# One row in 128 of an attention block given to POOL, and the masked-score pass one row earlier

## The chip, the cores and the metric

The kernel runs on one core of a Trainium2 chip. The metric is device time in microseconds of one execution, as the median of several runs. The engines are TensorE (PE in the profile), VectorE (DVE), ScalarE (ACT) and GpSimd (POOL); SyncE (SP) issues the DMAs.

## The reference

Four graph layers run one after the other on 8 graphs of 2048 nodes with 128 features, each with a residual and a layer norm. Layers 0, 2 and 3 multiply by a normalised adjacency matrix of 2048x2048. Layer 1 is the costly one, an attention whose score is a sum over features of a ReLU of a sum:

```python
q = x @ WQ
k = x @ WK
h = jax.nn.relu(q[:, None, :, :] + k[:, :, None, :])
score = jnp.einsum('bijd,d->bij', h, p)
att = jax.nn.softmax(score + mask, axis=-1)      # mask: 0 where adj > 0, else -1e22
return jnp.matmul(att, x)
```

For each graph and each of the 2048 rows i, a whole array of 128 features by 2048 nodes j must be formed (q plus one column of k, ReLU) and summed over the features with the weights p.

## The kernel before

The features lie on the 128 partitions, the nodes j along the free dimension. A graph is a batch b, and its rows i go in 16 blocks t of 128. A block has 32 groups g, and a group has four rows u, 128x2048 elements each. A group belongs to one engine: 20 groups of a block to VectorE (kind "D", line 658, a maximum of `q_pair` and one column of `k_pair`), 12 to ScalarE (kind "A", line 446, a ReLU of `q_f32` plus a column of `k_f32`). Groups 0, 1, 3, 4, 6, 8, 9, ... 28, 30 are VectorE's; groups 2, 5, 7, ... 29, 31 are ScalarE's.

`q_pair` holds two half-precision numbers in the place of one float, a high and a low part of q times |p|; the maximum is taken on the pair as one float. Each engine writes into a ring of two groups (`ring`). TensorE (line 891) sums each finished group over the partitions into `score` in PSUM, four chunks of 512 columns, with 32 multiplications for a D group and 16 for an A group. `rows_ready` counts finished groups, `rows_used` groups that TensorE is done with, so that an engine may write its group n+2 only when TensorE has used group n.

When the last group (31) of a block has been multiplied, VectorE reads the scores: `masked_scores` (lines 597 to 614) makes four passes (line 608, one for each chunk) that add the mask, which lies in `att`, and take the row maximum; then `row_max` (612) and `neg_max` (614). `bank_scored` counts the chunks that TensorE has finished, `scores_read` the chunks that VectorE has read. TensorE may start the next block's group 0 in a chunk only when it was read. ScalarE waits for `neg_max` ahead of its exponential (line 428), which stands ahead of its group 5. TensorE turns the weights at groups 4, 8, 12 and 16 (line 783), ScalarE and, in the tail only, VectorE copy them, and TensorE multiplies them by x at groups 10, 14, 18 and 22 (line 864). VectorE forms the next mask at group 24 (595), the inputs of the layer norm at group 26 (624 to 635) and the output at group 30 (639). Between those two POOL takes the root (`att_root`, lines 368 and 370).

The order within the engines is written out by hand. The pass over block t-1's scores stands inside block t, at a place given as (group, row):

```python
MASKED_AT, EXP_AT, NORM_AT, OUTPUT_AT = (1, 2), 5, 26, 30
```

so VectorE writes the four rows of group 0 and two of group 1, then reads the scores, then goes on. The first block of a batch has no such pass, and the last block's is in `att_tail`.

Of the kernel before, what the change touches and what calls it, by code (L numbers as in the profile page):

```python
# [9 lines left out]
ALU = mybir.AluOpType  # L10
# [19 lines left out]
def build(nc, x, adj, w0, b0, wq, wk, p, w2, b2, w3, b3, out):  # L30
# [31 lines left out]
    with ExitStack() as ctx:  # L62
        def sb(name, shape, dt=F32):
            return ctx.enter_context(nc.sbuf_tensor(name, shape, dt))

        def sem(name):
            return ctx.enter_context(nc.semaphore(name))
# [42 lines left out]
        rstd = sb("rstd", [P, PER])  # L110
        plus_half = sb("plus_half", [P, 1])
        ones = sb("ones", [P, 2])
        norm2 = sb("norm2", [P, 2])
        bound2 = sb("bound2", [P, 1])
        bound = sb("bound", [P, 1])
# [60 lines left out]
        rows_used = {"D": sem("vector_rows_used"), "A": sem("scalar_rows_used")}  # L176
        scores_read = sem("scores_read")
        mask_loaded = sem("mask_loaded")
        mask_ready = sem("mask_ready")
        bank_scored = sem("bank_scored")  # L180
        row_max_ready = sem("row_max_ready")
# [44 lines left out]
        TURN_AT = {4 + 4 * c: c for c in range(CHUNKS)}  # L226
        COPY_AT = {8 + 4 * c: c for c in range(CHUNKS)}
        MULTIPLY_AT = {10 + 4 * c: c for c in range(CHUNKS)}
        MASKED_AT, EXP_AT, NORM_AT, OUTPUT_AT = (1, 2), 5, 26, 30
        MASK_AT = 24  # L230

        def turned_beside(s):

# [103 lines left out]
        @block.gpsimd  # L337
        def _(pool):
            pool.memset(ident[:], 0.0).then_inc(ident_cleared, 1)
            pool.wait_ge(ident_cleared, 1)  # L340
            pool.affine_select(out=ident[:], in_=ident[:], compare_op=ALU.not_equal, fill=1.0, base=0,
                               pattern=[[-1, P]], channel_multiplier=1).then_inc(ident_ready, 1)
            pool.wait_ge(minus_half_ready, 1)
            pool.wait_ge(bound_ready, 2)
            pool.tensor_tensor(bound[:], bound2[:], plus_half[:], ALU.pow).then_inc(bound_ready, 1)
            pool.wait_ge(weights_loaded, 16 * 8)

            def graph_layer(b, stage, proj, xs, name):

                for k in range(2):  # L350
                    pool.wait_ge(turn_full[k], turn_use(b, proj, TURN_PROJ))
                for s in range(STEPS):
                    for j in range(PER):
                        t = s * PER + j
                        ins = pool.tensor_tensor(xs[:, t, :], xs[:, t, :], bias[name][:], ALU.add)
                    ins.then_inc(residual_biased, 1)
                for s in range(STEPS):
                    w = step_of(b, stage, s) + 1
                    pool.wait_ge(moments_ready, w)
                    settle(pool)  # L360
                    pool.tensor_scalar(var_eps[:], moments[:, :, 1], EPS, None, ALU.add).then_inc(variance_ready, 1)
                    pool.wait_ge(variance_ready, w)
                    pool.tensor_tensor(rstd[:], var_eps[:], minus_half[:, 0:PER], ALU.pow).then_inc(rstd_ready, 1)  # L363

            def att_root(n):
                pool.wait_ge(att_moments_ready, n)
                settle(pool)
                pool.tensor_scalar(att_var[:], att_mom[:, 1:2], EPS, None, ALU.add).then_inc(att_variance_ready, 1)  # L368
                pool.wait_ge(att_variance_ready, n)
                pool.tensor_tensor(att_rstd[:], att_var[:], minus_half[:, 0:1], ALU.pow).then_inc(att_rstd_ready, 1)  # L370

            with pool.Fori(0, B) as b:
                pool.wait_ge(degrees_ready, b + 1 + AHEAD)
                for i in range(GRAPH):
                    pool.tensor_tensor(dis[:, i, :], deg_sum[:, i, :], minus_half[:], ALU.pow).then_inc(roots_ready, 1)
                graph_layer(b, "layer0", "proj0", xin, "l0")
                with pool.Fori(1, T + 1) as t:
                    att_root(b * T + t)
                graph_layer(b, "layer2", "proj2", xatt, "l2")
                graph_layer(b, "layer3", "proj3", xatt, "l3")  # L380

# [127 lines left out]
        def _(dve):  # L509
# [87 lines left out]
            def masked_scores(n):  # L597

                dve.wait_ge(mask_ready, n)
                for c in range(CHUNKS):  # L600

                    if c < CHUNKS - 1:
                        dve.wait_ge(bank_scored, n * (CHUNKS - 1) + (c + 2 - CHUNKS))
                    else:
                        dve.wait_ge(rows_used[KIND[-1]], scored(n))
                    settle(dve)
                    part = att[:, c * BANK:(c + 1) * BANK]
                    nc.vector.tensor_tensor_reduce(out=part, in0=score[:, c, :], in1=part,  # L608
                                                   scale=1.0, scalar=-3.0e38, op0=ALU.add, op1=ALU.max,
                                                   accum_out=bank_max[:, c:c + 1]).then_inc(scores_read, 1)  # L610
                dve.wait_ge(scores_read, n * CHUNKS + CHUNKS)
                nc.vector.tensor_reduce(row_max[:], bank_max[:], AX.X, ALU.max).then_inc(row_max_ready, 1)
                dve.wait_ge(row_max_ready, n)
                nc.vector.tensor_scalar(neg_max[:], row_max[:], -1.0, None, ALU.mult).then_inc(neg_max_ready, 1)  # L614
# [27 lines left out]
            def att_block(b, t, before):  # L642
                n = b * T + t
                for g in range(GROUPS):
                    if before and g == NORM_AT:
                        norm_inputs(b, t - 1)
                    if before and g == OUTPUT_AT:
                        att_out(b, t - 1)
                    if g == MASK_AT:
                        mask(n)  # L650
                    if KIND[g] == "D":

                        dve.wait_ge(rows_used["D"], n * N_OF["D"] + (RANK[g] + 1))
                        for u in range(P // QUAD):
                            if before and (g, u) == MASKED_AT:
                                masked_scores(n)

                            ins = nc.vector.tensor_scalar(ring["D"][:, RANK[g] % RING * 4 + u, :], q_pair[:],  # L658
                                                          k_pair[:, bass.ds(t * P + (QUAD * u + g), 1)], None, ALU.max)
                        ins.then_inc(rows_ready["D"], 1)  # L660
# [97 lines left out]
        def _(pe):  # L758
# [3 lines left out]
            for kind in "AD":  # L762
                pe.sem_inc(rows_used[kind], RING)
            pe.sem_inc(scores_read, CHUNKS)
            for ahead in (att_output, out_stored, degrees_ready):
                pe.sem_inc(ahead, AHEAD)
            pe.wait_ge(ident_ready, 1)
            pe.wait_ge(w0_loaded, 16)
# [100 lines left out]
            def att_block(b, t, before):  # L869
                n = b * T + t  # L870
                for g in range(GROUPS):
                    kind = KIND[g]
                    if before and g in TURN_AT:
                        if TURN_AT[g] == 0:
                            pe.wait_ge(exp_ready, n)
                        turn_weights(b, t - 1, TURN_AT[g])
                    if before and g in MULTIPLY_AT:
                        weigh(b, t - 1, MULTIPLY_AT[g])
                    pe.wait_ge(rows_ready[kind], n * N_OF[kind] + (RANK[g] + 1))
                    window = unit_window if kind == "D" else sign_window  # L880
                    for c in range(CHUNKS):
                        if g == 0:

                            pe.wait_ge(scores_read, n * CHUNKS + (c + 1))
                        for part in range(2 if kind == "D" else 1):
                            for u in range(P // QUAD):
                                row = ring[kind][:, RANK[g] % RING * 4 + u, :]
                                row = halves(row)[:, c * BANK:(c + 1) * BANK, part] if kind == "D" else \
                                    row[:, c * BANK:(c + 1) * BANK]

                                ins = nc.tensor.matmul(score[QUAD * u:QUAD * (u + 1), c, :],  # L891
                                                       window[:, QUAD - 1 - g:2 * QUAD - 1 - g], row,
                                                       start=(g == 0 and part == 0), stop=(g == GROUPS - 1 and (kind == "A" or part == 1)),
                                                       tile_position=(0, QUAD * u))
                        if g == GROUPS - 1 and c < CHUNKS - 1:
                            ins.then_inc(bank_scored, 1)
                    ins.then_inc(rows_used[kind], 1)
# [61 lines left out]
```

## Time and profile before

| | |
|---|---|
| median of 3 runs | 15444.7 us (15443.2 to 15445.18) |
| profiled execution | 15425.52 us |
| its span, first to last instruction | 15423.3 us |
| mean granted TensorE clock | 0.974 of full speed |
| busy: TensorE, VectorE, ScalarE, POOL | 86%, 91%, 83%, 5% of the span |

The profile comes from one execution. Each instruction has a start and a duration; a group is all instructions of one line, engine, operation and pair of tiles, with the time for which its engine stood idle just ahead of them and who released it. A row's duration can overlap the next one's. TensorE's f32 multiplications appear as two records each.

### The profile page before, as it was taken

Reading aid. Unit: us, or ns where it says so; the run is one execution under the profiler, and the core shown is the slowest. Engines: PE = TensorE matmul, PEld = TensorE weight load, DVE = VectorE, ACT = ScalarE, POOL = GpSimd, SP = SyncE. Lnnn points to the kernel's source line nnn. Section 1 sums busy time; section 2 is a strip of 40 time slices with the busy share of each in tenths; the row PEclk is TensorE's granted clock in tenths of the full one; section 3 lists DMA queues with packets and bytes.
Section 4 is the critical chain, followed back from the end, with each engine's and each line's share of the span. In section 5 each row is a group of like instructions: output and inputs, shape, how many; then the busy total and the mean of one; then the engine's idle time right before and its main releaser. Section 6 shows DMA issues by size and latency. Waiting matters only on the chain. (4 is left out here: it accounts for less than half of the span.)

```text
span 15423.3 us, 363837 instructions
## 1 busy us (share of the span) xinstructions
PE 13297.8 (86%) x152965; PEld 6323.3 (41%) x152965; DVE 13958.6 (91%) x14776; ACT 12757.3 (83%) x7764; POOL 773.4 (5%) x863
## 2 busy tenths in 40 slices
PE   7888888888888888888888888888888888888888
PEld 4333453334533355333553335433354333543335
DVE  7999779997799977999779997899978999789996
ACT  6999769996699966999669996699966999679995
POOL 0000000000000000000000000000000000000000
PEclk9999999999999999999999999999999999999999
DMA  2000120001200012000120002100021000210001
GB/s 98 13 10 13 67 86 13 10 13 67 86 13 13 10 72 80 13 13 10 76 77 13 13 10 82 71 13 13 13 87 63 13 13 13 95 54 12 12 12 53
DMA packets 128454, 579.53 MB, mean 38 GB/s; under 512 B 27536, under 2 KB 61328, under 8 KB 61328
## 3 DMA queue, kind: packets, MB, share of 16 engines
q1 hardware_dynamic: 126864, 554.28, 9.4%
q8 instruction: 1492, 24.44, 0.6%
q14 instruction: 98, 0.80, 0.0%
HBM read 411.63 MB, written 142.61 MB: 36 GB/s over the span
## 5 line engine op out<-in xcount | busy, mean ns | idle before, releaser
L658 DVE TENSOR_SCALAR big<-q_pair,supp 128x2048 f32<-128x2048 f32 x10240 | 12302.8, 1280 | 42.7 <-PE score L891 35.8
L446 ACT ACTIVATE big<-q_f,k_f 128x2048 f32<-128x2048 f32 x6144 | 11758.2, 1996 | 694.1 <-PE score L891 681.4
L891 PE MATMUL score<-big,unit_window 128*32 128x512 f16 x81920 | 5335.8, 399 | 1773.9 <-DVE big L658 1522.6
L891 PE MATMUL score<-big,sign_window 128*32 128x512 f32 x49152 | 5615.4, 597 | 0.0
L891 PEld LDWEIGHTS score<-big,unit_window 128*32 128x32 bf16 x81920 | 2157.2, 97 | 4926.1 <-DVE big L658 2111.5
L891 PEld LDWEIGHTS score<-big,sign_window 128*32 128x32 f32 x49152 | 1607.8, 111 | 3113.6 <-issue 2832.1
L828 PE MATMUL acc<-supp,big 128*128 128x128 f32 x12288 | 1445.9, 275 | 30.3 <-ACT supp L402 29.0
L828 PEld LDWEIGHTS acc<-supp,big 128*128 128x128 f32 x12288 | 1406.4, 192 | 34.7 <-ACT supp L402 19.9
L386 ACT ACTIVATE x_turned<-turn 128x512 f32<-128x512 f32 x64 | 38.6, 603 | 1028.8 <-PE turn L783 971.6
L368 POOL TENSOR_SCALAR att_var<-att_mom 128x1 f32<-128x1 f32 x128 | 146.3, 1143 | 12870.3 <-DVE att_mom L635 12870.3
L556 DVE TENSOR_TENSOR agg<-acc,supp 128x512 f32<-128x512 f32 x64 | 44.3, 692 | 654.6 <-PE acc L828 654.6
L864 PEld LDWEIGHTS acc<-xin,att_turned 128*128 128x128 f32 x4096 | 505.2, 194 | 314.0 <-issue 313.4
L864 PE MATMUL acc<-xin,att_turned 128*128 128x128 f32 x4096 | 599.5, 290 | 2.4 <-DVE att_turned L385 2.4
L783 PE MATMUL turn<-ident,att 128*128 128x128 f32 x2560 | 418.3, 288 | 76.6 <-DVE big L385 46.4
L783 PEld LDWEIGHTS turn<-ident,att 128*128 128x128 f32 x2560 | 278.8, 143 | 402.7 <-issue 339.6
L386 ACT ACTIVATE big<-turn 128x512 f32<-128x512 f32 (+1 forms) x256 | 151.9, 593 | 342.1 <-PE turn L783 341.9
L428 ACT ACTIVATE att<-att,neg_max 128x2048 f32<-128x2048 f32 x128 | 256.5, 2004 | 175.8 <-DVE neg_max L614 172.0
L608 DVE CUSTOM_DVE_ANT_0 att<-score,att 128x512 f32<-128x512 f32 x512 | 324.0, 684 | 40.4 <-PE score L891 35.5
L385 DVE COPY big<-turn 128x512 f32<-128x512 f32 (+1 forms) x256 | 175.7, 686 | 169.1 <-PE turn L783 169.1
L433 ACT ACTIVATE att_turned<-turn 128x512 f32<-128x512 f32 x496 | 286.6, 578 | 45.5 <-PE turn L783 45.5
L370 POOL TENSOR_TENSOR att_rstd<-att_var,minus_half 128x1 f32<-128x1 f32 x128 | 276.3, 2159 | 10.7
L805 PE MATMUL acc<-w_l,x_turned 128*128 128x128 f32 x768 | 140.2, 342 | 119.4 <-DVE x_turned L385 111.8
(98 smaller groups left out, 2868.9 us busy)
## 6 DMA issues: line engine op xcount, KB each, us to landing
att<-in_adj_dram SPq DMA_DIRECT2D x160, 1024.0 KB, 4.8
adj_turned<-big SPq DMA_DIRECT2D x128, 1024.0 KB, 11.3
big<-adj_turned SPq DMA_DIRECT2D x128, 1024.0 KB, 18.0
q_f<-in_adj_dram SPq DMA_DIRECT2D x32, 1024.0 KB, 10.3
q_pair<-in_adj_dram SPq DMA_DIRECT2D x32, 1024.0 KB, 10.1
k_f<-in_adj_dram SPq DMA_DIRECT2D x32, 1024.0 KB, 10.4
xin<-in_x_dram SPq DMA_DIRECT2D x128, 64.0 KB, 1.8
out_dram<-xatt SPq DMA_DIRECT2D x32, 256.0 KB, 2.9
```

The lines of the kernel that those rows point to most:

```text
L370: pool.tensor_tensor(att_rstd[:], att_var[:], minus_half[:, 0:1], ALU.pow).then_inc(att_rstd_ready, 1)
L385: return nc.vector.tensor_copy(dst, turn[0][:])
L386: return nc.scalar.activation(dst, turn[1][:], ACT.Copy)
L428: nc.scalar.activation(att[:], att[:], ACT.Exp, bias=neg_max[:], accum_out=row_sum[:]).then_inc(exp_ready, 1)
L433: nc.scalar.activation(att_turned[:, k, :], turn[k][:], ACT.Copy).then_inc(turn_free[k], 1)
L446: ins = nc.scalar.activation(ring["A"][:, RANK[g] % RING * 4 + u, :], q_f32[:], ACT.Relu, bias=k_f32[:, bass.ds(t * P + (QUAD * u + g), 1)])
L608: nc.vector.tensor_tensor_reduce(out=part, in0=score[:, c, :], in1=part, scale=1.0, scalar=-3.0e38, op0=ALU.add, op1=ALU.max, accum_out=ba ...
L658: ins = nc.vector.tensor_scalar(ring["D"][:, RANK[g] % RING * 4 + u, :], q_pair[:], k_pair[:, bass.ds(t * P + (QUAD * u + g), 1)], None, A ...
L783: ins = nc.tensor.transpose(turn[k][:, j * P:(j + 1) * P], src(j), ident[:])
L828: ins = nc.tensor.matmul(acc[k][:, j * P:(j + 1) * P], big[:, t, m * P:(m + 1) * P], supp[:, m, :], start=(m == 0), stop=(m == T - 1))
L864: ins = nc.tensor.matmul(acc[0][:, 0:D], att_turned[:, k, j * P:(j + 1) * P], xin[:, c * PER + j, :], start=(c == 0 and j == 0), stop=(c = ...
L891: ins = nc.tensor.matmul(score[QUAD * u:QUAD * (u + 1), c, :], window[:, QUAD - 1 - g:2 * QUAD - 1 - g], row, start=(g == 0 and part == 0) ...
```

## The change

Row 3 of group 1 is left out of VectorE's list and written by POOL with a tensor-scalar operation (a minimum with 3.0e38, then a maximum with the column) into the same place in the ring. POOL first copies the column of `k_pair` to `pool_column`. In blocks 1 to 15 it waits for the first of the four masked-score passes (`scores_read`) before it writes the row, and then for the ring's place (`rows_used`). POOL's `att_root` for block t-1 comes behind the row of block t. TensorE waits for POOL's row ahead of group 1. `MASKED_AT` is (1, 1) in place of (1, 2).

```diff
+        pool_column = sb("pool_column", [P, 1])
...
-        MASKED_AT, EXP_AT, NORM_AT, OUTPUT_AT = (1, 2), 5, 26, 30
+        MASKED_AT, EXP_AT, NORM_AT, OUTPUT_AT = (1, 1), 5, 26, 30
         MASK_AT = 24
+        POOL_ROW = (1, 3)
...
+            def row(b, t, before):
+                n = b * T + t
+                g, u = POOL_ROW
+                pool.wait_ge(pool_row_ready, n + AHEAD)
+                settle(pool)
+                pool.tensor_copy(pool_column[:], k_pair[:, bass.ds(t * P + (QUAD * u + g), 1)]) \
+                    .then_inc(pool_column_ready, 1)
+                pool.wait_ge(pool_column_ready, n + 1)
+                if before:
+                    pool.wait_ge(scores_read, n * CHUNKS + 1)
+                    settle(pool)
+                pool.wait_ge(rows_used["D"], n * N_OF["D"] + (RANK[g] + 1))
+                settle(pool)
+                pool.tensor_scalar(ring["D"][:, RANK[g] % RING * 4 + u, :], q_pair[:], 3.0e38, pool_column[:],
+                                   ALU.min, ALU.max).then_inc(pool_row_ready, 1)
...
-                with pool.Fori(1, T + 1) as t:
+                pool.wait_ge(low_written, b * STEPS + STEPS)
+                pool.wait_ge(high_written, b * STEPS + STEPS)
+                row(b, 0, False)
+                with pool.Fori(1, T) as t:
+                    row(b, t, True)
                     att_root(b * T + t)
+                att_root(b * T + T)
...
+                            if (g, u) == POOL_ROW:
+                                continue
...
                     pe.wait_ge(rows_ready[kind], n * N_OF[kind] + (RANK[g] + 1))
+                    if g == POOL_ROW[0]:
+                        pe.wait_ge(pool_row_ready, n + 1 + AHEAD)
```

## Rows read from the trace of the kernel before


**Rows 1.** The page, part 1: busy time of each engine.
```profile
PE 13297.8 (86%) x152965; PEld 6323.3 (41%) x152965; DVE 13958.6 (91%) x14776; ACT 12757.3 (83%) x7764; POOL 773.4 (5%) x863
```

**Rows 2.** The page, part 5: groups; busy, mean ns | idle before, releaser.
```profile
L658 DVE TENSOR_SCALAR big<-q_pair,supp 128x2048 f32<-128x2048 f32 x10240 | 12302.8, 1280 | 42.7 <-PE score L891 35.8
L446 ACT ACTIVATE big<-q_f,k_f 128x2048 f32<-128x2048 f32 x6144 | 11758.2, 1996 | 694.1 <-PE score L891 681.4
...
L608 DVE CUSTOM_DVE_ANT_0 att<-score,att 128x512 f32<-128x512 f32 x512 | 324.0, 684 | 40.4 <-PE score L891 35.5
```

**Rows 3.** Timeline of VectorE, one block: start, us, line, operation [idle before].
```profile
2728.01 0.68 DVE L608 CUSTOM_DVE_ANT_0 att<-score,att 128x512 f32<-128x512 f32 x1
2728.62 0.08 DVE L608 DVE_READ_ACCUMULATOR2_ANT bank_max<- 128x1 f32 x1
...
2730.76 0.15 DVE L614 TENSOR_SCALAR neg_max<-row_max 128x1 f32<-128x1 f32 x1
2730.88 50.33 DVE L658 TENSOR_SCALAR big<-q_pair,supp 128x2048 f32<-128x2048 f32 x42
2781.49 14.44 DVE L658 TENSOR_SCALAR big<-q_pair,supp 128x2048 f32<-128x2048 f32 x12 [0.28 <-PE score L891]
...
2807.78 0.18 DVE L635 BATCH_NORM_AGGREGATE att_mom<-att_stats 128x2 f32<-128x6 f32 x1 [0.15 <-DVE att_stats L632]
2808.00 9.66 DVE L658 TENSOR_SCALAR big<-q_pair,supp 128x2048 f32<-128x2048 f32 x8
...
2817.83 12.04 DVE L658 TENSOR_SCALAR big<-q_pair,supp 128x2048 f32<-128x2048 f32 x10
2829.79 0.68 DVE L608 CUSTOM_DVE_ANT_0 att<-score,att 128x512 f32<-128x512 f32 x1
```

**Rows 4.** Waits of VectorE, the loop of the second batch (15 blocks).
```profile
DVE big L658 <- PE score L891: 4.5, 15, 0.3
```

**Rows 5.** Timeline of TensorE, end of the block before 2728.01.
```profile
2718.44 4.57 PE L891 MATMUL score<-big,sign_window 128*32 128x512 f32 x32
...
2724.65 3.63 PE L891 MATMUL score<-big,sign_window 128*32 128x512 f32 x32
```

**Rows 6.** Timeline of ScalarE around two masked-score passes.
```profile
2723.20 7.70 ACT L446 ACTIVATE big<-q_f,k_f 128x2048 f32<-128x2048 f32 x4 [4.99 <-PE score L891]
2730.94 2.01 ACT L428 ACTIVATE att<-att,neg_max 128x2048 f32<-128x2048 f32 x1
...
2832.73 2.00 ACT L428 ACTIVATE att<-att,neg_max 128x2048 f32<-128x2048 f32 x1 [1.69 <-DVE neg_max L614]
```

**Rows 7.** Timeline of TensorE ahead of the gap at 2781.49.
```profile
2766.91 2.00 PE L891 MATMUL score<-big,unit_window 128*32 128x512 f16 x32 [0.52 <-DVE big L658]
...
2779.32 3.99 PE L891 MATMUL score<-big,unit_window 128*32 128x512 f16 x64
```

**Rows 8.** Groups of POOL by shape; columns as in rows 2.
```profile
L368 POOL TENSOR_SCALAR att_var<-att_mom 128x1 f32<-128x1 f32 x128 | 146.3, 1143 | 12870.3 <-DVE att_mom L635 12870.3
L355 POOL TENSOR_TENSOR xatt<-xatt,bias_l 128x128 f32<-128x128 f32 x256 | 106.2, 455 | 104.3 <-PE turn L783 104.3
...
L341 POOL TENSOR_SCALAR_AFFINE_SELECT ident<-ident 128x128 f32<-128x128 f32 x1 | 0.3, 292 | 0.2 <-POOL ident L339 0.2
L339 POOL MEMSET ident<- 128x128 f32 x1 | 0.2, 204 | 0.3 <-POOLq L946 0.3
...
L946 POOL MEMSET const-float32-0.0<- 128x1 f32 x1 | 0.1, 98 | 0.2 <-issue 0.2
```

**Rows 9.** Timelines of POOL: in the block, and behind the last block.
```profile
2808.16 1.20 POOL L368 TENSOR_SCALAR att_var<-att_mom 128x1 f32<-128x1 f32 x1 [98.23 <-DVE att_mom L635]
2809.45 2.27 POOL L370 TENSOR_TENSOR att_rstd<-att_var,minus_half 128x1 f32<-128x1 f32 x1
...
15275.09 0.22 POOL L368 TENSOR_SCALAR att_var<-att_mom 128x1 f32<-128x1 f32 x1 [30.98 <-DVE att_mom L635]
```

**Rows 10.** Timeline of VectorE, the start of the second batch's first block.
```profile
2114.88 6.07 DVE L658 TENSOR_SCALAR big<-q_pair,supp 128x2048 f32<-128x2048 f32 x5 [0.35 <-ACT supp L467]
```

More of the change, by code:

```diff
@@ L178, in build @@
         mask_loaded = sem("mask_loaded")
+        pool_column_ready = sem("pool_column_ready")
+        pool_row_ready = sem("pool_row_ready")
         mask_ready = sem("mask_ready")
@@ L764, in _ @@
             pe.sem_inc(scores_read, CHUNKS)
-            for ahead in (att_output, out_stored, degrees_ready):
+            for ahead in (att_output, out_stored, degrees_ready, pool_row_ready):
                 pe.sem_inc(ahead, AHEAD)
```

## The prediction

> **What bounds the kernel now.** I read the busy table first. VectorE is busy for 91% of the span, TensorE for 86% and ScalarE for 83% [rows 1], so no single row names the bound. The groups do: L658, the attention rows on VectorE, holds 12302.8 us of 15423.3, and its idle time is 42.7 us in all [rows 2]. L446, ScalarE's share of the same work, is busy 11758.2 us and has idled 694.1.
>
> The timeline of one block shows it whole [rows 3]. From one first masked-score pass (2728.01) to the next (2829.79) is 101.78 us, and VectorE has one gap of 0.28 us that is owed to TensorE. That gap is at 2781.49, behind 42 rows. The waits over one batch's loop say the same: 4.5 us in 15 blocks for L658, no row for L608 [rows 4]. So the masked-score pass never waits in the loop, and a block is as long as VectorE's list of work. What the change takes from that list is gained in full, unless another engine is next in line within the saving.
>
> **What one row is worth.** 42 rows take 50.33 us. A row's shown time is 1.28, and it overlaps the next by 0.08, so the pitch is (50.33 - 0.08) / 42 = 1.196 us. The 10 rows in 12.04 us give the same. There are 128 blocks; 120 of them have the masked pass in them, 8 are the first of a batch.
>
> **The masked scores one row earlier.** Before, six rows stand ahead of the first pass and 42 between its end and the gap. After, five stand ahead, and behind it VectorE does 48 - 5 - 1 = 42 again. So the stretch from neg_max to the gap keeps its length and its balance against TensorE, and the row is lost between the gap and the pass. I check that whoever feeds the pass is early enough:
> - TensorE's scores. The last pass (the fourth) needs the end of group 31, at 2724.65 + 3.63 = 2728.28 [rows 5]. It starts at 2728.01 + 3 x 0.61 = 2729.84. The slack is 1.56 us, and 0.36 after the shift. This is a tight block: group 29, two ahead, took 4.57 us where group 31 took 3.63. Price: nothing, but the cover is thin; if I reckon half the blocks so tight, a quarter of a microsecond of lateness in each would cost 15 us.
> - ScalarE's exponential. In the tight block ScalarE ends four rows at 2730.90 and starts the exponential at 2730.94, just as neg_max is there (2730.91). In the next it has waited 1.69 us for neg_max [rows 6]. After the shift the tight blocks have the exponential up to 1.2 us late against VectorE. ScalarE takes such a lag: it waited 4.99 us ahead of its four rows in that block, so it is late nowhere for good, and its rows lie ready before TensorE takes them. Price: nothing.
> - The gap itself. From 2766.91, when VectorE has released a group, TensorE works without a pause to the pair of groups that starts at 2779.32 [rows 7], and VectorE, with 12 rows for that time, waits 0.28. Both ends move together with VectorE, so it stays 0.28.
>
> **POOL's column copy.** One 128x1 copy per block, issued after the last block's att_root, so some 20 us ahead of need. Its nearest rows are the 128x1 operations of att_root: 0.22 us alone, but 1.20 and 2.27 us beside VectorE's rows [rows 8, 9]. VectorE's rows beside them keep their pitch: the 8 rows that hold them take 9.66 us [rows 3], the same 1.196. So POOL waits and VectorE pays nothing. att_root itself comes on POOL's queue behind the row and some 77 us later; nothing else is queued there.
>
> **POOL's row, the term that decides.** No row of before shows POOL at 128x2048. From below: its 128x128 memset takes 204 ns against 98 for 128x1, so (204 - 98) / 127 = 0.83 ns an element, or 1.71 us for 2048, and 0.22 us of fixed cost as its 128x1 tensor-scalar: 1.93 us. From above: the 128x128 add with two inputs, 455 ns, gives (455 - 220) / 127 = 1.85 ns an element and 4.01 us. Between them the affine select, one input, 292 ns: at most (292 - 98) / 127 = 1.53 ns and 3.35 us, at the least (292 - 220) / 127 = 0.57 ns [rows 8]. The new operation has one tensor input, streams it and compares twice, with no arithmetic to speak of. I take 1.93 us, since the select's own spread reaches to either side of it, and keep 4.01 for the range.
>
> The Trainium skill, GPSIMD Engine Reference, section 3, counts 1.03 cycles an element for bodies of up to two operations, which would give 1.76 + 0.22 = 1.98 us, an estimate. By its measured 4497 ns for a two-input add of 2048 elements the change would be a loss.
>
> **When it runs and whom it holds up.** It may start when the first pass has been counted, 2728.62 + 0.08 = 2728.70. POOL starts 0.20 us after the release in att_root (2807.96 to 2808.16) [rows 3, 9]; here there is a second wait, for which I add 0.1: start 2729.0, end 2730.93. VectorE meanwhile runs three passes, row_max and neg_max (2730.76), and starts rows again at 2730.88. Whether those passes hinder POOL no row shows. That the rows do is shown: 0.22 us becomes 1.20. I take it that the converse holds for a long operation, so that neg_max or the next row waits till POOL is done. The overhang is 0.05 us if only the row is held and 0.17 if neg_max is; with a little for release I take 0.15. TensorE's new wait for POOL's row, ahead of group 1, is over long before VectorE's last row of that group (about 2733), so it costs nothing.
>
> The Trainium skill, SBUF, section "Who interferes with whom", says that a two-port VectorE operation and any GpSimd operation exclude each other, and that the second to issue waits for the whole instruction; passes with one SBUF input do not contend. The trace agrees for short POOL operations. By this rule the overhang is charged to VectorE in full, as I do.
>
> **The first block of each batch** has no pass to hide behind. VectorE starts rows at 2114.88, 0.35 us after its release [rows 10], and POOL then copies its column and takes its turn between rows. VectorE saves 1.20 and stands still for 1.93: a loss of 0.73, eight times 5.9 us.
>
> **The sum.** 120 x (1.196 - 0.15) = 125.5; less 5.9 gives 119.6 us. The profiled execution took 15425.5 us (span 15423.3), so it would be 15305.9. The median of the runs is 15444.7, 19.2 above it, and what is saved is saved there too: 15325.
>
> **The rivals.**
> - POOL's row is slow (the side of a loss). With 3.35 us it ends at 2732.35, an overhang of 1.5 against 1.2 saved: +0.35 x 120 + 2.15 x 8 = +59 us, 15504. With 4.01 us: +1.00 x 120 + 2.81 x 8 = +142 us, 15587. It decides from about 3.0 us on. For it speaks that POOL's only operations with input cost over 0.8 ns an element if their fixed part is small; against it, that 0.22 us of each is shown as fixed. 16 in 100.
> - POOL's row takes 2.3 to 2.9 us: 0.4 to 1.1 us of overhang, a gain of 20 to 90 us, about 15390. 10 in 100, 3 of them within 0.2%.
> - The passes contend as the rows do. POOL then begins between two passes and the next stands still for 1.93: +0.73 x 120 + 6 = +94 us, 15539. The passes read one operand from PSUM, and L608's idle time in the loop is nothing, but POOL was idle then too; so the trace is silent. By the skill's rule above it does not happen. 5 in 100.
> - Another engine takes up the saving: the fourth pass waits for TensorE in the tight blocks, or the ring stalls more. Half a row lost in half the blocks would leave 15360; the whole saving lost leaves 15445. 7 in 100, 4 of them within 0.2%.
> - The forecast, 15295 to 15375: 62 in 100.
>
> **How the numbers follow.** 0.2%, about what a measurement of this kernel can tell from no change, is 31 us. Faster: 62 + 7 + 3 = 72. Within: 3 + 4, and 2 of the slow rows near 3 us: 9. Slower: 14 + 5 = 19. The range begins at 15292, where POOL's row costs nothing in any block (128 x 1.196 = 153). At the top it must take in the gains cut short and the start of the slow rows: 15470 leaves about 18 in 100 out. The likeliest case's own range is 15295 to 15375.
>
> **What would show it.** L658 x10112, and POOL x128 at 128x2048 with a mean near 1.9 us. First pass to first pass 100.7 to 100.8 us in the loop. Idle time before L658's first row behind neg_max, or a neg_max longer than 0.15, of 0.1 to 0.3 us, with POOL's row as the neighbour. Still no idle time of L608 in the loop, the gap at 0.28. POOL's row over 3 us, or passes farther apart than 0.61, would make me wrong.

## The result: no gain, and slightly slower

| | before | after |
|---|---|---|
| median of 20 runs | 15444.42 us (15433.31 to 15453.47) | 15467.38 us (15453.75 to 15474.25) |
| ratio, 95% interval | | 1.0015 (1.0008 to 1.0022) |
| span of the profiled execution | 15423.3 us | 15463.7 us |
| mean granted TensorE clock | 0.974 | 0.962 |

I had forecast 15325. The change costs 0.15%; the 95% interval leaves out no change, and the cost is within the 0.2% that I called none. 15467 lies 3 us inside the top of my outer range, 15470, which I had put there for slow rows on POOL. That it reaches this far is luck: the cause is another one. The profiled execution of the kernel before is 19 us shorter than its median, that of the changed kernel 1.5 us.

The page of the changed kernel, part 5, with the columns of [rows 2, 8]:

```profile
L473 ACT ACTIVATE big<-q_f,k_f 128x2048 f32<-128x2048 f32 x6144 | 11756.0, 1997 | 826.3 <-PE score L922 823.9
L687 DVE TENSOR_SCALAR big<-q_pair,supp 128x2048 f32<-128x2048 f32 x10112 | 12180.4, 1281 | 199.2 <-PE score L922 191.6
...
L384 POOL TENSOR_SCALAR big<-q_pair,pool_column 128x2048 f32<-128x2048 f32 x128 | 258.5, 2019 | 2810.8 <-DVE bank_max L635 2808.4
...
L635 DVE CUSTOM_DVE_ANT_0 att<-score,att 128x512 f32<-128x512 f32 x512 | 323.6, 681 | 42.9 <-PE score L922 37.7
```

VectorE writes 128 rows fewer, 12180.4 us in place of 12302.8. POOL's row, the operation of unknown cost, takes 2.02 us in the mean; I had taken 1.93. So the parts cost what I said, and yet nothing is gained: L687's idle time has gone from 42.7 to 199.2 us, and nearly all of it waits for TensorE. The timeline of VectorE in one block of the loop, from 2733.50 to 2835.93, shows where:

```profile
2733.50 0.67 DVE L635 CUSTOM_DVE_ANT_0 att<-score,att 128x512 f32<-128x512 f32 x1
2734.11 0.07 DVE L635 DVE_READ_ACCUMULATOR2_ANT bank_max<- 128x1 f32 x1
...
2736.24 0.15 DVE L641 TENSOR_SCALAR neg_max<-row_max 128x1 f32<-128x1 f32 x1
2736.37 2.48 DVE L687 TENSOR_SCALAR big<-q_pair,supp 128x2048 f32<-128x2048 f32 x2
2739.80 24.01 DVE L687 TENSOR_SCALAR big<-q_pair,supp 128x2048 f32<-128x2048 f32 x20 [0.94 <-PE score L922]
2764.55 24.01 DVE L687 TENSOR_SCALAR big<-q_pair,supp 128x2048 f32<-128x2048 f32 x20 [0.74 <-PE score L922]
2788.82 14.44 DVE L687 TENSOR_SCALAR big<-q_pair,supp 128x2048 f32<-128x2048 f32 x12 [0.27 <-PE score L922]
...
2825.17 10.85 DVE L687 TENSOR_SCALAR big<-q_pair,supp 128x2048 f32<-128x2048 f32 x9
2835.93 0.68 DVE L635 CUSTOM_DVE_ANT_0 att<-score,att 128x512 f32<-128x512 f32 x1
```

The block is 102.43 us long, in place of 101.78 [rows 3]. The old gap ahead of group 19 is still there and still 0.27, at 2788.82. Two new ones have come: 0.94 ahead of group 3 (2739.80), two rows behind the masked-score pass, and 0.74 ahead of group 11 (2764.55), 20 rows later. POOL's row lies where it should, and VectorE's next row starts on time behind neg_max. The timeline of POOL:

```profile
2734.56 1.97 POOL L384 TENSOR_SCALAR big<-q_pair,pool_column 128x2048 f32<-128x2048 f32 x1 [17.94 <-DVE bank_max L635]
```

Now TensorE in the same stretch, from group 28 to the next block's group 6:

```profile
2722.61 3.48 PE L922 MATMUL score<-big,unit_window 128*32 128x512 f16 x32 [2.75 <-DVE big L687]
2725.86 3.79 PE L922 MATMUL score<-big,sign_window 128*32 128x512 f32 x32
2729.47 1.99 PE L922 MATMUL score<-big,unit_window 128*32 128x512 f16 x32
2731.28 3.61 PE L922 MATMUL score<-big,sign_window 128*32 128x512 f32 x32
2735.95 1.54 PE L922 MATMUL score<-big,unit_window 128*32 128x512 f16 x24 [1.05 <-DVE bank_max L635]
2739.00 2.46 PE L922 MATMUL score<-big,unit_window 128*32 128x512 f16 x40 [1.51 <-issue]
...
2749.51 3.11 PE L922 MATMUL score<-big,unit_window 128*32 128x512 f16 x32 [2.21 <-DVE big L687]
2752.40 4.17 PE L922 MATMUL score<-big,sign_window 128*32 128x512 f32 x32
2756.39 1.99 PE L922 MATMUL score<-big,unit_window 128*32 128x512 f16 x32
```

Group 28 takes 3.48 us and group 4 (2749.51) takes 3.11, where a group of 32 f16 multiplications otherwise takes 2.0. The windows view has both stretches, each with the one ahead of it. Its columns are the window and its length, then the busy time (and number of instructions) of TensorE's multiplications, its weight loads, VectorE, ScalarE and POOL, then the granted clock as a share of full speed (PEclk), the DMAs' busy share and GB/s:

```profile
2717.80:2722.60 4.80, 2.04 (x32) 0.85 (x32) 4.80 (x5) 4.80 (x3) 0.00 (x0) 1.00 0.00 0
2722.60:2726.10 3.50, 3.49 (x36) 1.54 (x40) 3.50 (x4) 2.28 (x2) 0.00 (x0) 0.53 0.00 0
2744.70:2749.50 4.80, 2.60 (x40) 1.18 (x36) 4.80 (x5) 4.80 (x4) 0.00 (x0) 1.00 0.00 0
2749.50:2753.00 3.50, 3.49 (x36) 1.38 (x40) 3.50 (x4) 3.50 (x3) 0.00 (x0) 0.59 0.02 5
```

The clock is at 0.53 and 0.59 of full speed there, so for most of each stretch at the lower of its two levels, 1.2 GHz. Just before each, TensorE had waited for VectorE for 2.75 and 2.21 us.

**The same stretch in the kernel before.** In the profiled execution of before, the low stretch at group 28 was there as well, ahead of 74 of the 120 passes in the loops, and cost next to nothing. The timeline of TensorE before, in the block of [rows 5], with rows not shown there:

```profile
2715.93 2.75 PE L891 MATMUL score<-big,unit_window 128*32 128x512 f16 x32 [2.79 <-DVE big L658]
...
2729.41 1.75 PE L891 MATMUL score<-big,unit_window 128*32 128x512 f16 x25 [1.13 <-DVE bank_max L608]
2732.21 0.63 PE L891 MATMUL score<-big,unit_window 128*32 128x512 f16 x7 [1.04 <-issue]
```

Set side by side, this is a race between two engines that both start when VectorE has released group 28. TensorE works off groups 28, 29, 30 and 31 and then the next block's group 0, whose place in the ring VectorE needs for its group 3. VectorE writes groups 30, 0 and 1 with the pass in between. Before: TensorE 2715.93 to 2732.84, 16.9 us; VectorE 2715.93 to 2733.28, 17.4. VectorE loses by 0.44 and waits for nothing. After: TensorE 2722.61 to 2739.63 (its last eight multiplications of group 0 start at 2739.00 and take 0.63, as before), 17.0; VectorE 2722.61 to 2736.37 + 2.48 = 2738.85, 16.2. TensorE loses, and VectorE waits 0.94. The row taken from VectorE was taken from its side of this race.

A part of TensorE's side is no work. Between its 24th and 32nd multiplication of group 0 it stands idle for 1.04 us before and 1.51 after (2737.49 to 2739.00), although the fourth part of the scores had been read by 2736.02. The profile calls that idle time "issue". It ends 3.9 and 4.1 us after the last group of the block, so it goes with TensorE's end of group 31 and not with the pass. The loop of TensorE turns between these two groups; that the jump causes the idle time was not tested.

**A block with the clock up at the group 28 ahead of it** in the changed kernel, the first in the loop of the second batch: 2226.22 to 2326.81 is 100.59 us, which is 101.78 less one row's 1.19. There is one gap, the old one, in the timeline of VectorE:

```profile
2226.22 0.68 DVE L635 CUSTOM_DVE_ANT_0 att<-score,att 128x512 f32<-128x512 f32 x1
...
2229.10 50.33 DVE L687 TENSOR_SCALAR big<-q_pair,supp 128x2048 f32<-128x2048 f32 x42
2279.71 14.44 DVE L687 TENSOR_SCALAR big<-q_pair,supp 128x2048 f32<-128x2048 f32 x12 [0.28 <-PE score L922]
...
2326.81 0.68 DVE L635 CUSTOM_DVE_ANT_0 att<-score,att 128x512 f32<-128x512 f32 x1
```

Of the 112 block times in the loops read this way, the middle half lies between 102.1 and 102.5 us in the changed kernel; 95 blocks have the gap at group 3, and the shortest of the other 17 take 100.6. Read for all 120 passes of the loops, the traces tie the gap to the clock: of the groups 28 of the changed kernel, 103 took 2.8 us or more, and 102 of these are followed by a gap at group 3; 17 took at most 2.05 us, and none of them is. Before, 74 took 2.5 us or more, and three were followed by a gap, of 0.1 us each.

### The profile page after: what moved, and what is told of

It is laid out like the page before. It is cut to its first block and busy times, and to the rows that moved or that the text cites. A ratio compares the mean times of both kernels' runs of the same rounds, so it can differ in the third digit from the quotient of the medians.

```text
span 15463.7 us, 364726 instructions
## 1 busy us (share of the span) xinstructions
PE 13406.0 (87%) x152965; PEld 6348.7 (41%) x152965; DVE 13837.2 (89%) x14648; ACT 12740.9 (82%) x7764; POOL 1042.0 (7%) x1119
## 5 line engine op out<-in xcount | busy, mean ns | idle before, releaser
L687 DVE TENSOR_SCALAR big<-q_pair,supp 128x2048 f32<-128x2048 f32 x10112 | 12180.4, 1281 | 199.2 <-PE score L922 191.6
L922 PE MATMUL score<-big,unit_window 128*32 128x512 f16 x81920 | 5419.9, 407 | 1699.5 <-DVE big L687 1419.2
L922 PEld LDWEIGHTS score<-big,unit_window 128*32 128x32 bf16 x81920 | 2189.2, 98 | 4864.4 <-DVE big L687 1850.4
L583 DVE TENSOR_TENSOR agg<-acc,supp 128x512 f32<-128x512 f32 x64 | 44.2, 691 | 655.2 <-PE acc L857 655.2
L384 POOL TENSOR_SCALAR big<-q_pair,pool_column 128x2048 f32<-128x2048 f32 x128 | 258.5, 2019 | 2810.8 <-DVE bank_max L635 2808.4
## 6 DMA issues: line engine op xcount, KB each, us to landing
big<-adj_turned SPq DMA_DIRECT2D x128, 1024.0 KB, 17.4
```

What stands on the lines that cost most here:

```text
L384: pool.tensor_scalar(ring["D"][:, RANK[g] % RING * 4 + u, :], q_pair[:], 3.0e38, pool_column[:], ALU.min, ALU.max).then_inc(pool_row_ready, 1)
```

## Experiments

The first question was whether TensorE's clock takes the saving, or POOL. Each ratio is to the kernel before as timed alongside, with its 95% interval; its medians there were 15445.86 us (e1 to e4), 15442.95 (e5 to e8) and 15439.17 (e9 to e12).

**e1_row_dropped.** POOL's part is taken out, and VectorE skips the row in blocks 1 to 15.

```diff
-                row(b, 0, False)
...
-                    row(b, t, True)
...
-                            if (g, u) == POOL_ROW:
+                            if before and (g, u) == POOL_ROW:
                                 continue
```

> The changed kernel without POOL's row: in blocks 1 to 15 of a batch row 3 of group 1 is computed by nobody (TensorE reads what an earlier group left in that place), in block 0 VectorE writes it. The masked-score pass stands at (1, 1). Theory A (TensorE's granted clock falls in more blocks and at a place where VectorE then waits for it; POOL has no part in it): 15455 to 15475 us, like the changed kernel, with VectorE waiting some 190 us for TensorE ahead of its rows. Theory B (POOL's row, by the ports or its semaphores, costs what it saves): 15295 to 15330 us.

Measured: 15456.06 us, ratio 1.0005 (0.9995 to 1.0014). In the groups view of VectorE, the row group waits for TensorE for 193.6 us:

```profile
L683 DVE TENSOR_SCALAR big<-q_pair,supp 128x2048 f32<-128x2048 f32 x10120 | 12174.7, 1279 | 200.2 <-PE score L916 193.6 <-ACT supp L490 2.4
```

One row in 80 is simply not computed, nobody does it in its place, and the kernel is no faster. So neither POOL's row nor its semaphores take the saving. They could account for 11 us at the most, by which this median lies below the changed kernel's.

**e2_pass_moved_only.** The other half of the change alone, on the kernel before.

```diff
-        MASKED_AT, EXP_AT, NORM_AT, OUTPUT_AT = (1, 2), 5, 26, 30
+        MASKED_AT, EXP_AT, NORM_AT, OUTPUT_AT = (1, 1), 5, 26, 30
```

> The kernel before with the masked-score pass at (1, 1) and all 80 rows on VectorE. Theory A: VectorE comes to group 3 when it did before, so the ring has its old slack and low clock stretches stay free: 15435 to 15455 us. Theory C (the earlier pass itself costs, by TensorE's scores or by the exponential): 15460 us or more.

Measured: 15451.61 us, 1.0006 (0.9996 to 1.0015), the same as before. Its profiled execution (span 15461.9) is not wholly calm, though: VectorE waits 66.3 us for TensorE where it waited 35.8 [rows 2], and 29 of the 120 blocks have a gap at group 3. This execution is the longest of the ten; whether the earlier pass uses up slack, or the kernel before has such executions too, one trace of each can't tell.

**e3_after_filled** and **e4_before_filled.** TensorE is given something to do in the gaps ahead of groups 4 and 28; the result, in the bank acc1 that the attention doesn't use, is read by nobody. All the work of the reference is done.

```diff
+        FILL = {4: 8, 28: 13}
...
+                    if before:
+                        for _ in range(FILL.get(g, 0)):
+                            nc.tensor.transpose(acc[1][:, 0:P], ident[:], ident[:])
                     pe.wait_ge(rows_ready[kind], n * N_OF[kind] + (RANK[g] + 1))
```

> The changed kernel with TensorE kept busy where it idled: 8 transposes of the identity into a free bank ahead of group 4 and 13 ahead of group 28 (about 1.3 and 2.1 us, in gaps of 2.2 and 2.8 us). Theory A: the granted clock stays at its upper level at these two places, a block takes 100.6 us, and the kernel 15300 to 15340 us. Theory B: no gain, 15455 to 15480 us.

> The kernel before with the same filling of TensorE. Theory A: its low clock stretches delayed nobody, so removing them gains nothing: 15435 to 15455 us. If filling helps by itself in another way, this run gets faster by the same amount as the filled changed kernel.

Measured: the changed kernel 15277.02 us, 0.9892 (0.9876 to 0.9909); the kernel before 15414.94, 0.998 (0.997 to 0.999). Both lie 20 us or more below what was expected for them by theory A. TensorE does more work, and the changed kernel is now 1.1% faster than the kernel before. The timeline of TensorE in e3 ahead of group 28:

```profile
2791.42 2.00 PE L926 MATMUL score<-big,unit_window 128*32 128x512 f16 x32 [0.81 <-DVE big L688]
2793.35 1.64 PE L911 MATMUL acc<-ident 128*128 128x128 f32 x13
2796.21 1.10 PE L926 MATMUL score<-big,unit_window 128*32 128x512 f16 x16 [1.22 <-DVE big L688]
```

And the windows view of e3 for the 3.5 us from group 28 on, columns as above:

```profile
2796.20:2799.70 3.50, 3.49 (x48) 1.48 (x52) 3.50 (x4) 2.28 (x2) 0.00 (x0) 1.00 0.00 0
```

The 13 transposes (1.64 us) leave a gap of 1.22 us in place of 2.75, and behind it the clock is at its upper level, 2.4 GHz. VectorE's block, in its timeline of e3, has one gap left, and is 100.59 us long (2807.09 to 2907.68):

```profile
2807.09 0.68 DVE L636 CUSTOM_DVE_ANT_0 att<-score,att 128x512 f32<-128x512 f32 x1
...
2809.97 50.33 DVE L688 TENSOR_SCALAR big<-q_pair,supp 128x2048 f32<-128x2048 f32 x42
2860.57 14.45 DVE L688 TENSOR_SCALAR big<-q_pair,supp 128x2048 f32<-128x2048 f32 x12 [0.27 <-PE score L926]
...
2907.68 0.68 DVE L636 CUSTOM_DVE_ANT_0 att<-score,att 128x512 f32<-128x512 f32 x1
```

With the clock out of the way, the change is worth 15414.94 - 15277.02 = 138 us, somewhat more than the 119.6 that I had summed. The filled kernel before has no shorter blocks in the loop than the plain one. Of its gain of 31 us, some 10 lie in the last blocks of the batches, between 1.5 and 1.9 us in six of the eight, as its profile shows. The other 20 are about the distance between the profiled execution of before, 15425.5, and its median; the one trace that there is of before cannot show them. The list of its runs points at the clock: of the 25 timed with e1 to e4, the 8 with a mean granted clock of 0.970 or 0.971 took 15445 to 15461 us, the 3 with 0.974, the clock of the profiled one, 15432 to 15436. So in a typical execution of the kernel before, the low stretches probably do cost some 20 us. That is not shown block by block.

**e5_fill_28_only** and **e6_fill_4_only** take the fillings apart.

```diff
+        FILL = {28: 13}        # e6: {4: 8}
```

> The changed kernel with only the 13 transposes ahead of group 28. If the low stretch at group 4 follows from VectorE's stall at group 3 (which the one at group 28 causes), both go and the time is that of the kernel filled in both places, 15270 to 15290 us. If the two are independent, the stall of 0.7 us ahead of group 11 stays in most blocks: 15325 to 15350 us.

> The changed kernel with only the 8 transposes ahead of group 4. The low stretch at group 28 and the stall of some 0.9 us ahead of group 3 should stay, the one ahead of group 11 should go: 15365 to 15400 us. If the stall ahead of group 3 does not come from the low stretch at group 28, this run is as fast as the kernel filled in both places, about 15277.

Measured: 15278.45 us, 0.9894 (0.9878 to 0.9911), and 15373.13, 0.9957 (0.994 to 0.9973). Filling group 28's gap is all that is needed. The low stretch at group 4 is a consequence of the first: when VectorE stalls ahead of group 3, TensorE waits longer for group 4. In e5's trace no low stretch is left at either place. The waits view of e6 has what is left of L687's 191.6 us:

```profile
DVE big L688 <- PE score L926: 115.5, 195, 1.6
```

**e7_row_dropped_filled.** As e1, with the filling.

> Filled in both places, and row 3 of group 1 computed by nobody in blocks 1 to 15 (VectorE writes it in block 0). It shows what POOL's row costs once the clock is out of the way. If VectorE is held up by the 0.15 us a block that the prediction charged: 18 us faster than the filled changed kernel, 15255 to 15265 us. If the row is wholly behind the pass: within 5 us of 15277, but for block 0, where POOL's row may cost some us either way.

Measured: 15277.7 us, 0.9894 (0.9877 to 0.9911). It equals e3 within a microsecond. POOL's row is hidden in the loop, and I had charged 0.15 us a block for nothing.

**e8_row_beside_rows.** As e3, but POOL's row does not wait for the pass.

```diff
-                if before:
-                    pool.wait_ge(scores_read, n * CHUNKS + 1)
-                    settle(pool)
```

> Filled in both places, and POOL's row no longer waits for the first masked-score pass, so that it starts beside VectorE's rows of group 1. If POOL's long operation holds VectorE's rows up for its whole length, VectorE stands still for some 1.9 us ahead of one row of each block: 15480 to 15520 us. If POOL only uses gaps between rows, as its 128x1 operations seem to, VectorE's rows keep their pitch and the time is about 15277 us, with a POOL row longer than 2.02.

Measured: 15279.94 us, 0.9896 (0.988 to 0.9913), no change against e3. POOL's row now takes 5.31 us, 5.13 in the mean, and VectorE's rows keep their pitch. The timeline of POOL in e8 around one pass:

```profile
699.23 5.31 POOL L381 TENSOR_SCALAR big<-q_pair,pool_column 128x2048 f32<-128x2048 f32 x1 [13.48 <-PE score L922]
```

And that of VectorE in e8:

```profile
702.61 0.68 DVE L632 CUSTOM_DVE_ANT_0 att<-score,att 128x512 f32<-128x512 f32 x1
...
705.06 0.08 DVE L632 DVE_READ_ACCUMULATOR2_ANT bank_max<- 128x1 f32 x1
...
705.37 0.15 DVE L638 TENSOR_SCALAR neg_max<-row_max 128x1 f32<-128x1 f32 x1
705.49 1.29 DVE L684 TENSOR_SCALAR big<-q_pair,supp 128x2048 f32<-128x2048 f32 x1
```

POOL was issued beside the rows, at 699.23, and ended at 704.54. The first pass started at 702.61, so if POOL's row got nowhere before it, it ran for 1.93 us from there, about as long as undisturbed (1.97). In the first block of a batch, which has no pass, it went otherwise. The timeline of VectorE in the changed kernel, at the start of the second batch:

```profile
2122.89 7.79 DVE L687 TENSOR_SCALAR big<-q_pair,supp 128x2048 f32<-128x2048 f32 x5 [0.35 <-ACT supp L494]
```

And that of POOL:

```profile
2123.39 2.61 POOL L384 TENSOR_SCALAR big<-q_pair,pool_column 128x2048 f32<-128x2048 f32 x1 [0.30 <-POOL pool_column L375]
```

Five rows take 7.79 us there, in place of 6.07 [rows 10]: VectorE was held up for 1.72 us by POOL's 2.61, and the other seven batches show the same loss within 0.1 us. So both things happen, VectorE being held and POOL being kept waiting. Which one wins where was not settled. Neither case is POOL's row in the gaps between rows.

**e9_filled_elsewhere.** The control for the filling: as many transposes, but ahead of groups 22 and 25.

```diff
+        FILL = {22: 5, 25: 8}
```

> The changed kernel with 13 transposes as well, but ahead of groups 22 and 25 (5 and 8), where TensorE also waits for VectorE and no low clock stretch was seen. If it matters that TensorE is busy just ahead of group 28, the low stretches and both stalls stay: 15440 to 15475 us. If any added work in the block does, 15275 to 15300 us.

Measured: 15468.69 us, 1.002 (1.001 to 1.0029), like the changed kernel, with 196.9 us of VectorE's rows waiting for TensorE. It is the place that counts.

**e10_pass_kept.** The changed kernel with the pass back at (1, 2).

```diff
-        MASKED_AT, EXP_AT, NORM_AT, OUTPUT_AT = (1, 1), 5, 26, 30
+        MASKED_AT, EXP_AT, NORM_AT, OUTPUT_AT = (1, 2), 5, 26, 30
```

> The changed kernel with the masked-score pass left where it was, at (1, 2); POOL's row stays behind its first part. VectorE comes to group 3 at the same time as in the changed kernel, so if the stall is between group 28 on TensorE and group 3 on VectorE, moving the pass has no part in it: 15450 to 15480 us. If the earlier pass is what takes the saving back, 15310 to 15340 us.

Measured: 15473.82 us, 1.0023 (1.0013 to 1.0033), with 197.6 us of waits. Moving the pass is not what causes the stall of the changed kernel.

**e11_fill_28_small.** Five transposes ahead of group 28 in place of 13.

> The changed kernel with 5 transposes ahead of group 28 in place of 13 (0.8 us of a gap of 2.8). How little is enough: 15275 to 15300 us if the clock then holds, 15440 to 15475 if it still falls in most blocks, between them if it falls in some.

Measured: 15417.89 us, 0.9987 (0.9978 to 0.9997), with 153.2 us of waits in place of 191.6. A little work in the gap saves the clock in some blocks only.

**e12_filled_turn_later.** The old gap of 0.28 us, on top of e5.

```diff
-        TURN_AT = {4 + 4 * c: c for c in range(CHUNKS)}
+        TURN_AT = {4: 0, 8: 1, 12: 2, 17: 3}
```

> The changed kernel with 13 transposes ahead of group 28 and the fourth turning of the weights on TensorE ahead of group 17 in place of 16. What is left is the stall of 0.28 us in each of 120 blocks ahead of group 19, which waits for TensorE's group 16; 0.58 us of turning taken from ahead of that group should end it, 34 us less than 15278: 15240 to 15250 us. If the stall has another cause, or comes back one group later, 15270 to 15285.

Measured: 15236.67 us, 0.9871 (0.9855 to 0.9888), the fastest of all, 1.3% below the kernel before. The row group in the groups view of VectorE:

```profile
L688 DVE TENSOR_SCALAR big<-q_pair,supp 128x2048 f32<-128x2048 f32 x10112 | 12152.6, 1280 | 7.5 <-ACT supp L495 2.4 <-PE score L926 0.6
```

Of e5's 44.2 us of idle time ahead of the rows 7.5 are left. The gain is 41.8 us against e5 (the kernel before differs by 3.8 us between the two sets of runs), more than the 34 of the gaps and 3 us beyond the range expected: a row behind a gap also loses the 0.08 us by which it would have overlapped the one before it, and that is 10 us in 120 blocks.

## Why the prediction was wrong

**What bounds the kernel.** Right as a reading: VectorE has one gap in a block, and a block lasts as long as its list. With the clock up at group 28 a block of the changed kernel takes 100.59 us, 101.78 less the 1.196 of a row; I had forecast 100.7 to 100.8, with the overhang.

**The step that failed** is the check of "whoever feeds the pass". I looked at TensorE's scores for the pass, at ScalarE's exponential and at the gap ahead of group 19, and priced all three at nothing, which they were. I did not look at the fourth tie between the engines, the ring: VectorE's group 3 needs TensorE to be done with group 0. In the tight block that slack was 0.44 us, and it could be read from the timelines of TensorE and VectorE. The row removed was 1.2 us of VectorE's side of it. The prediction even says of the tight block that group 29 took 4.57 us in place of 3.63, and follows that delay to the pass and to ScalarE only. I also took the number of tight blocks as given, half of them; it was 74 of 120, and the change raises it to 103. Why it does is open.

**The rival that came true** is "another engine takes up the saving". I gave it 7 in 100 and named the ring's stalls in half a sentence; its price was to be at the most the whole saving, 15445. The result is 22 us beyond that, since the new stalls have a consequence of their own. In the block shown, 0.94 us at group 3 lengthens TensorE's wait ahead of group 4, the clock falls a second time, and 0.74 follows at group 11. Together that is 1.7 us, more than the row's 1.2. Filling only the gap ahead of group 4 (e6) takes this second stall away, leaves 74 gaps at group 3 in place of 102, and makes the kernel 94 us faster.

**The sum of the changed kernel** by measured terms: 128 rows less are 153 us. L687 idles 156.5 us more. Block 0 loses 1.72 x 8 = 14. The new stalls, 311 - 120 = 191 of them, each lose the overlap of 0.08, 15. That makes +33 us; the spans differ by 40.4, and the other 7 are not accounted for.

**POOL's row**: I took 1.93 us by the rate of the memset, and undisturbed it takes 1.97. Both rivals that made it slow, and the one in which the passes contend, are out: the passes keep their pitch of 0.61 beside it. The estimate of 1.98 us, from the figure for bodies of up to two operations in the Trainium skill, GPSIMD Engine Reference, section 3, and a fixed part of 0.22 us from [rows 9], agrees with 1.97; this operation has one tensor input, and the page's figure for two-input adds is not its price.

**The overhang**: 0.15 us charged, nothing measured (e7). Without it my sum would be 119.6 + 18 = 137.6 us, and e3 against e4 shows 138; block 0, forecast at 5.9 us and measured at 4.2, adds 1.7 to the sum. POOL's row ends at 2734.56 + 1.97 = 2736.53, 0.16 behind the start of VectorE's next row, and that row is not late; the overlap is 0.14 to 0.20 us in all 120 blocks of the loops. The Trainium skill, SBUF, section "Who interferes with whom", has the second to issue wait for the whole instruction. Block 0 agrees with it (1.72 us held), and so does the pitch of the passes, which read one operand from SBUF. The 5.31 us of POOL in e8 agree in that one of the two waits, but not in the order: two of VectorE's rows that began behind POOL's went ahead of it. The 0.16 us of overlap in the loop show no such wait, if POOL's times, which are rough in a profile, can be read that finely.

**Block 0**: a loss of 0.73 us forecast; 1.72 - 1.20 = 0.52 measured.

## What to carry to other kernels

When work is taken off the engine that sets the pace, list every semaphore between it and the next engine over one period and write down the slack of each, also in the period's worst version; the smallest slack, not the mean share of busy time, tells how much can be gained before the next engine holds the first one up, and here the stalls that followed cost more than the saving. If TensorE waits in bursts, look at the granted clock just behind its waits: a low stretch that costs nothing today is covered by slack that the next improvement will spend. Here the change alone lost 23 us, filling the waits alone gained 31, and both together gained 169; the same multiplications in other waits gained nothing.

## What the runs showed of the hardware

- The granted clock of TensorE fell to 1.2 GHz behind a wait of 2.75 us at group 28 and stayed up behind one of 1.22 (e3); with 5 transposes, 0.77 us of work in the gap, it fell in some blocks and not in others (e11). Group 28 took 3.48 us in place of 2.0 in the block shown.
- It did not fall behind every wait of this length: in the first block of the second batch TensorE waits 2.33 us ahead of group 28 and then works at full speed, and four blocks later, at 2622.02 in the changed kernel, it does so behind 2.79 us. Most blocks of the changed kernel settle at about 102.4 us, with the low stretches at the same place in block after block; what ties them to that rhythm was not tested.
- POOL's 128x2048 row beside VectorE's f32 rows took 5.31 us without slowing them in one place, and held one up for 1.72 us in another.
- At the turn of the loop TensorE stands idle, for 1.04 and 1.51 us in the two blocks shown, with nothing that the profile shows to wait for, and goes on some 4 us behind the end of its last group. This is part of the race that the change lost.
